# Hybrid block on one core: in projection and convolution of the second half issued within the first scan, routing of the first half within the second

## The reference, cut to what matters

```python
x = x + block_a(layernorm(x))          # Mamba + mixture of experts
x = x + ffn(layernorm(x)); x = x + attention(layernorm(x)); x = x + ffn(layernorm(x))

# block_a; x is (4, 512, 128), D_INNER 256, D_STATE 16, 4 taps, DT_RANK 64, 8 experts, top 2
xi, z = split(rmsnorm(x, rms1_w) @ in_proj_w)
xi = silu(depthwise_conv(xi) + conv_b)
dt, Bm, Cm = split(xi @ x_proj_w)
delta = softplus(dt @ dt_proj_w + dt_proj_b)
for t in range(512):                   # for each of 16 states n
    h = exp(delta[t] * A) * h + delta[t] * xi[t] * Bm[t]
    y[t] = (h * Cm[t]).sum(states)
y = (y + D_skip * xi) * silu(z)
x = x + y @ out_proj_w
w, sel = top_k(softmax(rmsnorm(x, rms2_w) @ router_w), 2)
x = x + sum over the two chosen experts of w * (silu(x @ Wg) * (x @ Wu)) @ Wd
```

## Time and profile before

| | us |
|---|---|
| median of three runs | 722.12 |
| lowest, highest | 720.75, 722.17 |
| the profiled execution, time | 728.63 |
| the profiled execution, span of the trace | 726.9 |
| granted TensorE clock, mean of the span | 0.927 |

### The profile page before, as it was taken

The page is one execution under the profiler, slowest core; times in us unless marked ns, Lnnn a source line. Parts: engine busy times, 40 slices in busy tenths (PEclk is TensorE's granted clock), DMA queues, the critical chain, the costliest instruction groups (busy, mean ns, idle before and its releaser), DMA issues.

```text
span 726.9 us, 11045 instructions
## 1 busy us (share of the span) xinstructions
PE 570.0 (78%) x3447; PEld 361.2 (50%) x3447; DVE 488.5 (67%) x1310; ACT 384.8 (53%) x604; POOL 331.7 (46%) x289
## 2 busy tenths in 40 slices
PE   1938667788467576798779999975779989989887
PEld 1413223244122232497779989952545545545456
DVE  5549999954798899635323475358877787886053
ACT  1586555525654455266346756732446666566731
POOL 5259989800799999132666532531111112111010
PEclk9978999899587998999889999995999999999999
DMA  5736456401387855120114200323203103000001
GB/s 142 278 114 191 156 168 177 127 0 35 128 256 208 243 178 170 32 69 16 42 46 115 86 19 15 100 76 84 54 9 84 30 2 96 12 2 2 2 14 46
DMA packets 50523, 65.91 MB, mean 91 GB/s; under 512 B 7730, under 2 KB 29250, under 8 KB 50210
## 3 DMA queue, kind: packets, MB, share of 16 engines
q1 hardware_dynamic: 45122, 59.27, 27.8%
q0 software_dynamic: 2496, 5.15, 1.9%
q10 hardware_dynamic: 2848, 0.78, 0.5%
HBM read 47.46 MB, written 9.52 MB: 78 GB/s over the span
## 4 chain that ended last, share of the span: by engine, by line
PE 40%; DVE 8%; issue 5%; ACT 4%; ACTq 1%; another core or an unknown queue 0%; POOL 0%; DMA 0%; POOLq 0%; DVEq 0%
PE ps L1507 37%; DVE arena L1427 3%; ACT arena L1056 2%; PE ps L1766 1%; DVE x L1362 1%; DVE nb L1155 1%; DVE stats L1142 1%; PE ps L1656 1%; PE ps L1773 1%; ACTq L1046 0%; ACT arena L1076 0%; ACT arena L1064 0%; ACT r L1056 0%; DVE mv L1145 0%
## 5 line engine op out<-in xcount | busy, mean ns | idle before, releaser
L1507 PE MATMUL ps<-arena 128*128 128x128 f32 (+11 forms) x2150 | 328.3, 330 | 45.2 <-DVE arena L1427 17.5
L1507 PEld LDWEIGHTS ps<-arena 128*128 128x128 f32 (+2 forms) x2150 | 211.7, 160 | 129.0 <-issue 57.2
L1507 PE MATMUL ps<-arena,ident 128*128 128x512 f32 x256 | 137.8, 685 | 69.4 <-DVE arena L1298 69.4
L1288 DVE TENSOR_TENSOR_SCAN arena<-ps,arena 128x512 f32<-128x512 f32 x128 | 147.8, 1202 | 9.2 <-POOL arena L821 6.3
L1427 DVE CUSTOM_DVE_ANT_0 arena<-ps,cmask 128x128 f32<-128x128 f32 (+3 forms) x256 | 111.5, 487 | 26.5 <-PE ps L1507 26.2
L821 POOL TENSOR_TENSOR arena<-arena 128x1024 f32<-128x1024 f32 x64 | 128.6, 2029 | 0.6
L997 ACT ACTIVATE ps<-arena 128x512 f32<-128x512 f32 x128 | 88.0, 690 | 76.2 <-DVE arena L1288 73.4
L1507 PEld LDWEIGHTS ps<-arena,ident 128*128 128x128 f32 x256 | 52.9, 219 | 150.8 <-DVE arena L1298 97.7
L1481 DVE TENSOR_TENSOR arena<-arena,ps 128x512 f32<-128x512 f32 x46 | 31.7, 688 | 78.0 <-PE ps L1507 41.0
L806 POOL DMA_INDIRECT moe_out<-arena,xT x46 | 45.5, 989 | 82.3 <-DVE arena L1451 71.6
L1056 ACT ACTIVATE arena<-ps 128x1024 f32<-128x1024 f32 (+3 forms) x86 | 57.0, 709 | 36.3 <-PE ps L1507 35.9
(11 more groups left out here) (191 smaller groups left out, 604.3 us busy)
## 6 DMA issues: line engine op xcount, KB each, us to landing
arena<-bc_rows SPq DMA_DIRECT2D x128, 256.0 KB
arena<-arena SPq DMA_DIRECT2D x64, 64.0 KB
arena<-arena SPq DMA_DIRECT2D x28, 128.0 KB, 2.5
moe_rows<-arena SPq DMA_DIRECT2D x2, 1495.0 KB, 11.8
arena<-moe_rows SPq DMA_DIRECT2D x8, 325.0 KB, 4.7
arena<-in_L_attn_a_Wg SPq DMA_DIRECT2D x8, 256.0 KB
arena<-in_L_attn_a_Wu SPq DMA_DIRECT2D x8, 256.0 KB
arena<-moe_out SPq DMA_DIRECT2D x4, 512.0 KB, 4.5
```

Of the source, the lines that this page charges most:

```text
L1288: V.tensor_tensor_scan(hst[:, g % STATES, e, :], bank(6 + e), dBx[:, g % RING, e, :], 0.0, ALU.mult, ALU.add).then_inc(s_scan, 1)
L1507: return T.matmul(o, l, rr, start=start, stop=stop)
```

## The change

Four things move or change; the arithmetic is the same but for where intermediate values lie.

1. In the first scan, TensorE does the in projection and the convolution of block 0 for sequences 2 and 3, one matmul or two taps at a time, all through PSUM bank 5 (`AHEAD`), and ScalarE copies each result out (`COPY_AT`): xi to `xip`, the convolution to `xc`, z to a new place `zr`. The Silus follow in the gap. The convolution of block 1 stays on VectorE, after the last weighing of the first scan and ahead of the second gate.
2. The out projection of the first half comes after the second half's x and dt projections on TensorE, and the residual, the moments and the small products come on VectorE between the two sums that form delta (`form_delta`, `add_residual`).
3. The routing of the first half goes into states 35 to 47 of the second scan (`ROUTE_AT`), and its sixteen scatters to the sixteen states of the second sequence of that half (48 to 63). The power -1/2 follows the product of state 34. Some small tiles (`ridf`, `nblk`, half of `req`) move to PSUM bank 4.
4. Relu of softplus is written back to the PSUM bank that it reads (banks 2 to 5), and Abs comes ahead of it; the sum that forms delta reads it there.

```diff
@@ tiles
+        z_at = at[0] - 11 * P - 2 * 3 * HID
+        zr = arena[:, z_at:z_at + CT * HL].rearrange("p (e l) -> p e l", e=CT)
-        ridf = carve([2, TH])
-        req = carve([2, TH, NE])
+        ridf = ps[:, 4, 64:64 + 2 * TH].rearrange("p (k t) -> p k t", k=2)
+        req = (ps[:, 4, 128:128 + TH * NE].rearrange("p (t e) -> p t e", t=TH), carve([TH, NE]))
-        nblk = carve([NE])
+        nblk = ps[:, 4, 96:96 + NE]
@@ schedule
+        DT = (2, 4)
+        AHEAD = {1: ("xi", 0, 0), 3: ("xi", 0, 1), 5: ("xi", 1, 0), 7: ("xi", 1, 1), 9: ("taps", 0, 0), 10: ("taps", 0, 1),
+                 13: ("z", 0, 0), 15: ("z", 0, 1), 17: ("taps", 1, 0), 18: ("taps", 1, 1), 21: ("z", 1, 0), 23: ("z", 1, 1)}
+        COPY_AT = {3: ("xi", 0, 0), 5: ("xi", 0, 1), 7: ("xi", 1, 0), 9: ("xi", 1, 1), 12: ("taps", 0, 1),
+                   15: ("z", 0, 0), 17: ("z", 0, 1), 20: ("taps", 1, 1), 23: ("z", 1, 0), 25: ("z", 1, 1)}
+        first_1 = NS * HB
+        ROUTE_AT = {"h2norm": first_1 + 3, "h2turn": first_1 + 4, "input": first_1 + 6, "router": first_1 + 7,
+                    "logits": first_1 + 9, "top_a": first_1 + 10, "exp": first_1 + 11, "top_b": first_1 + 12,
+                    "rank": first_1 + 13, "slots": first_1 + 15}
@@ SyncE: rows of B and C stored for each sequence
+                    if g == first:
+                        store_rows(HB * h)
+                        sp.wait_ge(s_bt, 16 * (HB * h + 1))
+                    elif g == first + BS:
+                        store_rows(HB * h + 1)
+                    elif g == first + NS:
+                        sp.wait_ge(s_bt, 16 * (HB * h + 2))
@@ GpSimd, in state n of sequence c of half h
-                        j = c * NS + n - 2
+                        if h and c == 0 and n == 2:
+                            powers(0, 2 * TB)
+                        j = c * NS + n - NS
                         if h and 0 <= j < 2 * TH:
                             scatter(0, j // 2, j % 2)
-                powers(2 * TB * h, 2 * TB)
+            powers(2 * TB, 2 * TB)
@@ ScalarE
+            def relu_abs(h, c):
+                for e in range(CT):
+                    act.wait_ge(s_dtp, 2 * (HB * h + c) + e + 1)
+                    last = S.activation(u[:, c, e, :], bank(DT[c] + e), ACT.Abs, bias=dtb[:, e:e + 1])
+                    S.activation(bank(DT[c] + e), bank(DT[c] + e), ACT.Relu, bias=dtb[:, e:e + 1])
+                ch.link(last)
+            def inputs_1():
+                act.wait_ge(s_cvc, HB)
+                act.wait_ge(s_zc, 2 * HB)
+                for c in range(HB):
+                    cs = slice(c * L, c * L + L)
+                    S.activation(xc[:, 0, cs], xc[:, 0, cs], ACT.Silu, bias=convb[:, 0:1]).then_inc(s_xc, 1)
+                for e in range(CT):
+                    for c in range(HB):
+                        cs = slice(c * L, c * L + L)
+                        S.activation(zr[:, e, cs], zr[:, e, cs], ACT.Silu).then_inc(s_zs, 1)
+                for c in range(HB):
+                    act.wait_ge(s_cd, HB + c + 1)
+                    S.activation(xc[:, 1, c * L:c * L + L], v[:, c, 1, :], ACT.Silu, bias=convb[:, 1:2]).then_inc(s_xc, 1)
+                    if c == 0:
+                        row_copy(1, 0)
+                S.preload_act_table_set("natural_log_exp_and_others")
+                relu_abs(1, 0)
+                row_copy(1, 1)
+                exp_log(0)
+                relu_abs(1, 1)
+                exp_log(1)
@@ ScalarE, after the decays and the copy of C in state g
+                        if g in COPY_AT:
+                            copy_ahead(*COPY_AT[g])
+                        if g == ROUTE_AT["input"]:
+                            moe_input(0)
+                            moe_input(1)
+                        if g == ROUTE_AT["logits"]:
+                            logits(0)
+                        if g == ROUTE_AT["exp"]:
+                            router_exp(0)
@@ VectorE
+            def form_delta(b):
+                c = b % HB
+                dve.wait_ge(s_u, b + 1)
+                V.tensor_tensor(delta[:, :, c * L:c * L + L], bank(DT[c], 2), u[:, c, :, :], ALU.add).then_inc(s_dl, 1)
...
+                else:
+                    form_delta(HB)
+                    add_residual(0)
+                    form_delta(HB + 1)
...
+                        if g == ROUTE_AT["h2norm"]:
+                            h2_norm(0, count["var"])
+                        if g == ROUTE_AT["top_a"]:
+                            top_a(0)
+                        if g == ROUTE_AT["top_b"]:
+                            top_b(0)
+                        if g == ROUTE_AT["slots"]:
+                            find_slots(0, rank_bank(0))
                 weigh(state_of(HB * h + HB, -1))
+                if h == 0:
+                    conv_1(HB)
+                    conv_1(HB + 1)
                 gate(HB - 1)
@@ TensorE
+            def inputs_1():
+                pe.wait_ge(s_wpc, NPREP)
+                pe.wait_ge(s_xc, 2 * HB + 3)
+                x_proj(1, 0)
+                dt_proj(1, 0)
+                pe.wait_ge(s_xc, 2 * HB + 4)
+                pe.wait_ge(s_zc, 2 * HB)
+                x_proj(1, 1)
+                dt_proj(1, 1)
+                out_proj(0)
+            def ahead(what, c, e):
+                if what == "xi":
+                    pe.wait_ge(s_dl, HB)
+                    wait(pe, s_xi, 2 * HB + 2 * c + e if c or e else 0)
+                    mm(bank(5), ipw[:, e * P:e * P + P], mamba_in(1, c)).then_inc(s_ip, 1)
...
@@ TensorE, after the sums of state g - 1
+                    if g in AHEAD:
+                        ahead(*AHEAD[g])
+                    if g == ROUTE_AT["h2turn"]:
+                        pe.wait_ge(s_dl, NB)
+                        turn_h2(0)
+                        turn_h2(1)
+                    if g == ROUTE_AT["router"]:
+                        router(0)
+                    if g == ROUTE_AT["rank"]:
+                        rank(0)
```

More of the change, by code:

```diff
@@ L990, in copy_c @@
+            for h in range(HB):
+                (inputs_0, inputs_1)[h]()
                 def copy_c(g):
@@ L1269, in _ @@
                 if h:
-                    top_a(h - 1)
-                if h:
-                    top_b(h - 1)
-                    find_slots(h - 1, rank_bank(h - 1))
+                    dve.wait_ge(s_sc[0], 16 * 2 * TH)
                 for c in range(HB):
-                    b = HB * h + c
-                    dve.wait_ge(s_u, b + 1)
-                    V.tensor_tensor(delta[:, :, c * L:c * L + L], v[:, c, :, :], u[:, c, :, :], ALU.add).then_inc(s_dl, 1)
+                    for j in range(TB):
+                        t = TB * (HB * h + c) + j
+                        last = V.tensor_scalar(nb[:, c, j, :], r[:, t, :], small[:, 2, t:t + 1], None, ALU.mult)
@@ L1279, in scan @@
+                    last.then_inc(s_h2, 1)
+            for h in range(HB):
+                if h == 0:
+                    for b in range(HB):
+                        conv_1(b)
+                    for b in range(HB):
+                        form_delta(b)
+                else:
+                    form_delta(HB)
+                    add_residual(0)
+                    form_delta(HB + 1)
                 def scan(g, e):
@@ L1582, in _ @@
-                for c in range(HB):
-                    b = HB * h + c
-                    pe.wait_ge(s_zs, 2 * b + 2)
-                    pe.wait_ge(s_xc, 2 * b + 2)
-                    if h and c:
-                        pe.wait_ge(s_rx, h)
-                    for e in range(CT):
-                        last = mm(ps[0:RK + 2 * NS, (4, 0)[c], :], xpw[:, e, :], xc[:, e, c * L:c * L + L],
-                                  start=(e == 0), stop=(e == CT - 1))
-                    last.then_inc(s_pj, 1)
```

233 lines of the change are left out of this document (118 added, 115 removed).

## The result

The changed kernel takes 725.20 us, the median of seven runs (722.07 to 726.80), against 721.85 for the kernel before, also seven runs. The ratio is 1.0051, 95% interval 1.0036 to 1.0067: slower by 3.35 us, where +3.5 was forecast. In a later group of runs the ratio was 1.0075 (1.0062 to 1.0088), or +5.4 us.

A forecast was written before the change was run, and what follows sets the result against it. VectorE was taken to set the pace in the first scan and states 48 to 63, GpSimd almost as full. Terms +0.35 - 20.15 + 6.55 + 15.0 + 1.7 = +3.45 us on 722.12 gave 725.6 us, range 718.3 to 730.3.

The forecast's parts named there:

- first scan with its front: First scan and the sums ahead of it: faster delta sum against ScalarE's ten copies, net +0.35 us (-0.95 to +4.8).
- gap: Between the two scans: 24.45 us where it was 44.6, so -20.15 us (-23.0 to -18.2).
- states 32 to 47: Second scan, first part: scatters leave, routing comes in, 62.95 us for 56.4, so +6.55 us (+2.6 to +9.6).
- states 48 to 63: Second scan, second part: GpSimd bounds it with sixteen scatters behind six weighings, 59.8 us against 44.8, +15.0 (14 to 16).
- end: Last sums after the second scan: TensorE's granted clock falls after idling some 3 us, +1.7 us (0 to 3.4).
- The two small products: Near the gap's end: VectorE products with two SBUF inputs wait for GpSimd products to end, 2.85 us.
- Rival A: Gap and routing: no small operation is locked out, 2.85 and 3.0 us go, total 719.7 us; chance 0.27.
- rival B: Only the gap's pair of small products is locked out, routing's 3.0 us goes, total 722.6 us; chance 0.15.
- collisions in the routing: States 32 to 47: normalisation, shift and top two each meet GpSimd once, 0 to 2.0 us each, 3.0 taken.
- The front's part: Ahead of the first scan: last sum forming delta reads one operand from PSUM, 0.95 us taken off.
- TensorE's added work: First scan: eight matmuls and two convolutions, hidden in TensorE's 28 us of idle time, costing nothing.
- Rival C: First scan: the ten copies aren't hidden, 5.7 us instead of 1.3, total 730.0 us; chance 0.13.

The follow-up runs named there:

- ctl_after: The changed kernel, unchanged, measured again in a later group: 725.81 us, ratio 1.0075 to the kernel before.
- a_power: Changed kernel with GpSimd's power -1/2 of the first half after state 32's product instead of state 34's: 733.65 us, ratio 1.0024 to the kernel before.
- b_scatter: Kernel before with only the scatters moved to the sixteen states of sequence 3, routing left in the gap: 739.31 us, ratio 1.0103.
- a_mid: Changed kernel with the first half's normalisation ahead of state 35's second scan on VectorE, not after it: 723.91 us, ratio 1.0034 to the kernel before.
- a_swap: Changed kernel with GpSimd's six weighings in sequence 2 and two in sequence 3, beside the scatters: 722.77 us, ratio 0.9871 to the kernel before.
- a_copies: Changed kernel with ScalarE's ten copies in states where VectorE weighs, TensorE's matmuls moved to match: 725.35 us, ratio 1.0072 to the kernel before.
- a_sched: As a_copies, but TensorE's work taken ahead never shares a state with a weight's preparation, last five copies moved too: 721.93 us, ratio 1.0018 to the kernel before.
- ctl_before: The kernel before, unchanged, run again for a second profile: 732.99 us in one run beside 732.11 for the others.
- b_relu: Kernel before with only softplus's Relu kept in PSUM and delta formed from there: 720.72 us, ratio 1.0003.

## Why the prediction was right, step by step

In us against the profile of before, with both profiles of after. The front is counted from VectorE's first sum for delta (43.09 us before, 43.39 and 43.47 after), since what lies ahead of it differs by 1.4 us between two executions of the kernel before:

| step | forecast | after | ctl_after |
|---|---|---|---|
| first scan with its front | +0.35 | +1.7 | +1.1 |
| gap | -20.15 | -19.7 | -20.6 |
| states 32 to 47 | +6.55 | +5.4 | +5.6 |
| states 48 to 63 | +15.0 | +15.5 | +15.4 |
| end | +1.7 | +2.8 | +1.7 |
| sum, to the last gate | +3.45 | +5.7 | +3.2 |

The medians differ by +3.35. The bulk of the step is thus what the forecast said: 20 us gained in the gap, and spent in the second scan. That the total agrees to 0.1 us is luck: single steps are off by up to 1.4 us, some too high and some too low, and two executions of the kernel after differ by 2.5. Of what is shown and what isn't:

**Gap.** The scan starts 24.9 us behind the last weighing (24.0 in ctl_after, the 0.9 lying ahead of the first delta), with 24.45 forecast. The two small products cost 2.46 us more than alone (0.88 + 1.92 - 0.34), where 2.85 was taken, each until the end of one GpSimd product as the prediction had it. a_power shows it by its reverse. The section "Who interferes with whom" of "SBUF — State Buffer" in the Trainium skill, which the prediction weighed, is borne out here for operations of eight columns. Rival A (719.7) is refuted by that, rival B (722.6) by the routing's rows.

**States 32 to 47.** VectorE's own work without scatters was taken as 50.7 and was 50.4 in b_scatter. The collisions in the routing cost 2.5 us where the middle of a range, 3.0, was taken; ScalarE's scalings cost 0.81 for 1.0; with 8.2 for the routing's own operations, as forecast, that makes the 61.9. What the prediction did not see is that the collisions belong to no one operation: moving one away brought another (a_mid), and more work for GpSimd there lengthened them (a_swap).

**States 48 to 63.** 59.8 forecast, 60.2 measured, by the same count: GpSimd's 3.22 us for a state with scatter, 2.35 for a weighing, and the lead lost while it waits for the slots (7.48 us of standing still). a_swap (-6.6) and b_scatter (+13.4 there) follow GpSimd's work. b_scatter also shows that GpSimd's lead would not have been enough without the routing: the stretch asks it for 65.6 us (16 x 3.22 + 6 x 2.35), 20.8 more than VectorE's 44.8, and three states of lead are 9.7.

**End.** Forecast +1.7 for a lower granted clock after idle time. The twelve last parts, in before and in after:

```profile
295.32 5.43 PE L1507 MATMUL ps<-arena,ident 128*128 128x512 f32 x12 [0.34 <-DVE arena L1298]
```

```profile
298.57 8.16 PE L1595 MATMUL ps<-arena,ident 128*128 128x512 f32 x12 [3.32 <-DVE arena L1398]
```

The granted clock over them is 1.00 in before, 0.66 in after, and 0.76 in ctl_after, where they took 7.11 us behind 2.39 of idle time (0.79 in the window shown there, which begins ahead of them). That is +2.8 and +1.7: the right mechanism, and a size that differs from one execution to the next, with the pause not telling which (a_copies has 6.81 us behind 3.31, a_sched 7.12 behind 3.61).

**First scan: the term that was mis-sized.** Net +0.35 was forecast, +1.1 to +1.7 came. The front's part was right: 0.95 taken for the faster sum, 0.9 found. The second sum, in before and in after:

```profile
47.57 2.32 DVE L1277 TENSOR_TENSOR arena<-arena 128x1024 f32<-128x1024 f32 x1 [3.26 <-ACT arena L989]
```

```profile
47.74 1.23 DVE L1341 TENSOR_TENSOR arena<-ps,arena 128x1024 f32<-128x1024 f32 x1 [3.12 <-ACT arena L984]
```

From the first sum to the scan it is 6.73 us in before, ctl_before and b_scatter, and 5.83 in after, ctl_after and b_relu. The scan itself took 2.6 and 2.0 us more where 1.3 was taken (1.8 to 2.6 in the five profiles with this placing). Of the 2.2 and 1.4 us for which VectorE waits for the decays, not all is the copies: before has 0.3 of such waits, and 1.1 put down to no engine, which after has hardly any of. All waits ahead of scans came to 1.5 us in before and to 3.0 and 2.3 in the two profiles of after, so the copies cost 1.5 and 0.8 by the waits. And TensorE's added work was costed at nothing, hidden in 28 us of idle time. It costs 0.6 in both profiles, because one place in the scan, the gate of the sequence, needs the sums at once and four buffers don't help it: 1.06 us of in projection stand ahead of them in state 15. The last 0.6 us is in none of these waits and wasn't traced. That a whole stage's idle time hides the work put into it is the step that failed; a_sched, in which the gate doesn't wait and the decays' waits come to 1.1 us, has 97.9. Rival C (730.0), which priced all copies as unhidden, at 5.7 us, is refuted by the same waits.

Why the medians stand at +3.35 and, in the later group, at +5.4 (0.0075 x 720.44) is not settled; the stages up to the gate give +5.7 in the earlier profile and +3.2 in the later, the other way round. Part of that is the choice of execution: the profiled one of after took 1.4 us more than its median, and that of ctl_after 1.8 less.

## What to carry to other kernels

When work moves out of a gap into a full stage, add it up for each engine of the stage that takes it, stretch by stretch; here the helper engine, not the main one, became the bound, and shifting four weighings to the stretch before was worth 13 us where the move itself had brought none: 6.6 in the full stretch, 1.9 in the one before it, and 2.7 to 3.8 at the end. A share that one engine does for another (`ON_POOL`) has to be set anew whenever either's other work moves. And idle time hides moved work only where nothing behind it in the queue is needed at once: look for the one consumer without a buffer, such as a gate at the end of a sequence.

## What the runs showed of the hardware

- An operation of VectorE with two SBUF inputs waits for the end of the operation that GpSimd is in, even a small one: 0.17 us became 0.88 and 1.92 for 128 x 8 elements. One that reads PSUM for one input does not (1.23 beside a product, b_relu).
- The normalisation, with one tensor input and a column of scalars, is held too: eight operations took 1.66 us with GpSimd idle, 3.37 when one of GpSimd's operations fell among them, and 6.21 when three did. I had expected one wait for the group; in a_swap it is held three times, once by each.
- A scatter's DMA issue takes GpSimd 1.01 us (1.22 the first), and 0.17 more before it; a state with one took 3.22 us for a product of 2.00.
- The granted clock behind a pause of TensorE is not set by the pause's length alone: four parts took 1.99 us behind 2.74 us of idle time in before, 3.39 at 0.58 behind 3.05 in a_copies, and the last sums ran at 0.76 behind 2.39 in ctl_after. I had priced such a fall only at the end.
